# Weights of the second half split early and parked in DRAM, unrolled sequences, norms on ScalarE

## The reference

```python
x = x + attention(layernorm(x))     # q, k with rotary embedding, causal softmax, output weights wo
x = x + ffn(layernorm(x))
# ffn, for a token row x:
scores = softmax(x @ gate_w.T); topk_w, topk_idx = top_k(scores, 2)     # weights scaled to sum 1
y_all  = (silu(x @ w1[e]) * (x @ w3[e])) @ w2[e]                        # the two chosen experts
y      = sum(y_sel * topk_w) + (silu(x @ sw1) * (x @ sw3)) @ sw2        # plus the shared expert
```

## Time and profile before

| | us |
|---|---|
| three timed runs | 816.66, 817.6, 818.66 (median 817.6) |
| the profiled execution | 822.53, its span 820.8 |
| one sequence of the loop | 74.9 |
| busy share of the span | PE 92%, PEld 86%, DVE 78%, ACT 65%, POOL 59% |

### The profile page before, as it was taken

One profiled execution on the slowest core, in us unless ns is written; L12 is line 12 of the kernel. 1 busy time (PEld: TensorE's weight loads), 2 busy tenths in 40 slices (PEclk: granted clock), 3 DMA queues, 4 the chain that ended last, 5 costly groups with the idle time before them and its releaser, 6 DMA issues.

```text
span 820.8 us, 17064 instructions
## 1 busy us (share of the span) xinstructions
PE 755.2 (92%) x5520; PEld 703.7 (86%) x5520; DVE 640.8 (78%) x1765; ACT 532.9 (65%) x1663; POOL 482.2 (59%) x508
## 2 busy tenths in 40 slices
PE   3799999998999999999999999999996979999994
PEld 3688999988999999899989999998895868888884
DVE  5698989976997988799889979987995474444457
ACT  3688777756776777677667767777887433555531
POOL 3678666656667676766666676667776361343410
PEclk9899999998999999999999999999999997999998
DMA  7253434353000000000000000000232212333354
GB/s 223 58 178 114 160 168 183 153 206 116 15 2 27 0 13 6 19 13 0 13 13 13 0 26 0 13 6 22 83 80 79 74 40 78 110 105 108 113 209 144
DMA packets 35723, 61.20 MB, mean 75 GB/s; under 512 B 6744, under 2 KB 27192, under 8 KB 35096
## 3 DMA queue, kind: packets, MB, share of 16 engines
q1 hardware_dynamic: 31624, 49.14, 17.8%
q0 software_dynamic: 4048, 11.42, 3.9%
HBM read 47.03 MB, written 32.46 MB: 97 GB/s over the span
## 4 chain that ended last, share of the span: by engine, by line
PE 58%; DVE 17%; POOL 11%; issue 6%; ACT 4%; DMA 4%; SPq 0%; POOLq 0%; DVEq 0%; ACTq 0%
PE bank L528 45%; DVE work L879 5%; POOL work L425 4%; PE bank L568 3%; POOL qkt_lo L1416 3%; PE bank L561 3%; DVE work L872 2%; PE bank L577 2%; PE bank L728 2%; DVE work L888 2%; POOL rows_by_expert L1529 2%; DVE pt_lo L900 1%; DMA stage<-in_L_attn_wk 1%; DMA rows_by_expert<-xn,slot 1%; PE bank L743 1%
## 5 line engine op out<-in xcount | busy, mean ns | idle before, releaser
L1416 POOL TENSOR_TENSOR qkt_lo<-work,qkt_hi 128x512 fp32r<-128x512 f32 x128 | 165.6, 1294 | 99.9 <-ACT qkt_hi L1233 94.8
L425 POOL TENSOR_TENSOR work<-work 128x512 f32<-128x512 f32 x127 | 165.1, 1300 | 76.0 <-DVE work L879 71.2
L879 DVE TENSOR_TENSOR work<-bank,sinn 64x512 f32<-64x512 f32 x256 | 176.1, 688 | 3.4
L1233 ACT CAST qkt_hi<-work 128x512 fp32r<-128x512 f32 x128 | 79.5, 621 | 110.5 <-POOL work L425 109.8
L528 PE MATMUL bank<-xnt_hi,w_lo 128*128 128x256 f32 x512 | 146.9, 287 | 3.2 <-POOL w_lo L1476 3.0
L528 PE MATMUL bank<-xnt_lo,w_hi 128*128 128x256 f32 x512 | 146.6, 286 | 0.0
L528 PE MATMUL bank<-xnt_hi,w_hi 128*128 128x256 f32 x512 | 146.6, 286 | 0.0
L1240 ACT ACTIVATE work<-work,bias 128x128 f32<-128x128 f32 (+1 forms) x256 | 112.6, 441 | 0.0
L872 DVE TENSOR_TENSOR work<-bank,cosn 128x512 f32<-128x512 f32 x128 | 88.0, 687 | 23.5 <-PE bank L528 23.4
L528 PEld LDWEIGHTS bank<-xnt_hi,w_lo 128*128 128x128 f32 x512 | 99.7, 195 | 3.9 <-DVE xnt_lo L910 3.3
L528 PEld LDWEIGHTS bank<-xnt_hi,w_hi 128*128 128x128 f32 x512 | 100.0, 195 | 0.0
(11 more groups left out here) (151 smaller groups left out, 2181.7 us busy)
## 6 DMA issues: line engine op xcount, KB each, us to landing
rows_by_expert<-in_zero_t SPq DMA_DIRECT2D x8, 2056.0 KB
stage<-rows_by_expert SPq DMA_DIRECT2D x39, 128.5 KB, 2.1
stage<-in_L_ffn_w SPq DMA_DIRECT2D x32, 88.0 KB, 2.0
rows_by_expert<-in_zero_t SPq DMA_DIRECT2D x2, 1028.0 KB
resid<-in_L_attn_x SPq DMA_DIRECT2D x8, 256.0 KB, 3.9
stage<-in_L_attn_wq SPq DMA_DIRECT2D x8, 256.0 KB, 3.6
stage<-in_L_attn_wk SPq DMA_DIRECT2D x8, 256.0 KB, 4.3
stage<-in_L_attn_wv SPq DMA_DIRECT2D x8, 256.0 KB, 4.2
```

What stands on the lines that cost most here:

```text
L425: eng.tensor_tensor(roped[:, a], rope_cos[:, a], rope_sin[:, a], ALU.add).then_inc(rope_add, 1)
L879: op = nc.vector.tensor_tensor(rope_sin[lo:lo + 64, a], p_qk[a][hi:hi + 64, :, :], sn, ALU.mult)
L1233: nc.scalar.copy(qkt[a][0][:, :, :], roped[:, a]).then_inc(qkt_hi, 1)
L1416: nc.gpsimd.tensor_tensor(qkt[a][1][:, :, :], roped[:, a], qkt[a][0][:, :, :], ALU.subtract).then_inc(qkt_lo, 1)
```

## The change

- The 30 pieces of the second half's weights are split in sequences 0 to 5, one in each of the heads 10 to 14 of sequence 0 and of the heads 0, 1, 3, 4, 5 of sequences 1 to 5. The high and the low part go into two of the five staging slots (one buffer for each part), all low parts on POOL, and SP stores both into a DRAM tensor `w_d` (`keep`). ACT waits for the stores of a piece before it makes the high part of the next. The staging buffer has three slots for raw pieces then.
- In sequence 7 SP loads the split weights from `w_d` as the groups of attention weights become free.
- SP clears the scatter region once in each sequence.
- The loop is gone: sequences 1 to 7 are written out on all engines.
- Both norms are made on ACT, as `x * rstd + shift`, in head 9 and head 3. POOL makes `shift` behind its `rsqrt` in heads 6 and 2.
- Shared tiles 0 and 1 run in heads 12 to 15 of sequence 7, with the first product of tile 2. `S1` is 10, so tiles 3 to 9 come before the experts and 10 to 15 behind. Other PSUM banks are used; `silu` and product share a buffer. `finish` is called for two tiles in each late shared tile. Some `nop`s are dropped.

```diff
-S1 = 8
+S1 = 10
+        w_d = nc.dram_tensor("weights_split", (2, NU * DC + 2 + E, P, CH), F32, kind="Internal").ap()
+        parts = [stage[:, RAW + b, :].bitcast(F32R) for b in range(2)]
...
+            heads = [(FIRST, h) for h, k in enumerate([3, 2, 3] + [2] * 6) for _ in range(k)]
+            heads += [(FIRST, h) for h in range(10, N - 1)]
+            heads += [(b, h) for b in range(1, B - 2) for h in (0, 1, 3, 4, 5)]
...
+            def keep(k):
+                sp.wait_ge(w_lo[1], lo_count(NATT + k + 1, 1))
+                for b in range(2):
+                    sp.dma_start(w_d[b, k], stage[:, RAW + b, :]).then_inc(kept, 16)
+                if k % 5 == 4:
+                    b = k // 5 + 1
+                    sp.wait_ge(qk_ps, b * N + 4)
+                    clear(b)
...
 # ACT
             def split_hi(n):
                 _, seen = pieces[n]
-                act.wait_ge(staged[n % NSTAGE], staged_count[n])
+                if n == NATT:
+                    wait_pieces(act, NATT)
+                if n > NATT:
+                    act.wait_ge(kept, 32 * (n - NATT))
+                act.wait_ge(staged[slot_of(n)], staged_count[n])
...
+                        if h == 12:
+                            silu_s(0)
+                            rows_high(1)
...
+                        if h == 14:
+                            silu_s(1)
+                            high_s(0)
+                        if h == 15:
+                            silu_s(2)
+                            rows_high(3)
+                            high_s(1)
+                    elif h == 9:
+                        norm_x(b + 1)
                     if b is not FIRST:
+                        if h == 3:
+                            rows_norm(b, b - 1)
...
 # POOL
+            def shifts(k, done_sem, count, step_sem, n):
+                nc.gpsimd.tensor_scalar(shift[:, k, :], mv[:, :, 0], -1.0, 1.0, ALU.mult, ALU.mult).then_inc(step_sem, 1)
+                pool.wait_ge(step_sem, 2 * n - 1)
+                pool.wait_ge(done_sem, count)
+                nc.gpsimd.tensor_tensor(shift[:, k, :], shift[:, k, :], rstd[:, :], ALU.mult).then_inc(step_sem, 1)
...
 # PE, in the heads of the last sequence
-                    if b is LAST and h >= 14:
-                        up_s(0, h - 14)
+                    if b is LAST:
+                        if h == 12:
+                            up_s(0, 0)
+                        if h == 13:
+                            up_s(0, 1)
+                            up_s(1, 0)
+                        if h == 14:
+                            turn_s(0)
+                            up_s(1, 1)
+                        if h == 15:
+                            up_s(2, 0)
+                            turn_s(1)
...
-            sequence(1)
-            with pool.Fori(2, LAST) as b:
+            for b in range(1, B):
                 sequence(b)
-            sequence(LAST)
```

More of the change, by code:

```diff
@@ L167, in build @@
         assert DCONST <= D - 2 * NJ
-        room = work[:, e0:2816]
+        room = work[:, 2048:2816]
         past = room[:, 0:NJ * E].rearrange("p (j e) -> p j e", j=NJ)
@@ L411, in split_now @@
         def split_now(b, h):
-            which = "first" if b is FIRST else "last" if b is LAST else None
-            return plan.get((which, h), [])
-        FIRST, LAST = 0, B - 1
+            return plan.get((b, h), [])
         def wait(eng, s, value):
@@ new lines, in _, with units_in @@
+            for k in range(NP - NATT):
+                if k >= RAW:
+                    keep(k - RAW)
+                piece_in(NATT + k)
+            for k in range(NP - NATT - RAW, NP - NATT):
+                keep(k)
+            sp.wait_ge(qk_ps, (LAST - 1) * N + 4)
+            clear(B - 1)
+            clear(B)
+            sp.wait_ge(cleared, 16 * (B + 1))
+            sp.dma_start(xs_d[E * REGION:XROWS, :], zero_t[E * S:, :]).then_inc(cleared, 16)
+            def units_in(lo, hi, done):
+                for u in range(lo, hi):
+                    for b in range(2):
+                        src = w_d[b, DC * u:DC * (u + 1), :, 0:UW].rearrange("c p m -> p c m")
+                        sp.dma_start(ups[b][:, u].bitcast(F32), src).then_inc(done, 16)
@@ new lines, in free @@
+            def free(g):
+                sp.wait_ge(qk_ps, LAST * N + (g + 1) * GH)
+                sp.wait_ge(v_ps, LAST * 2 * G + 2 * (g + 1))
+            sp.wait_ge(kept, 32 * (NP - NATT))
+            free(0)
+            units_in(0, 2, ups_in)
+            rows_in(0)
+            units_in(2, 4, experts_in)
+            free(1)
+            units_in(4, 8, experts_in)
+            free(2)
+            units_in(8, NU, experts_in)
+            k0 = NU * DC
+            for b in range(2):
+                for n in range(SB):
+                    r = min(P, SI - n * P)
+                    src = w_d[b, k0 + n // 2, 0:r, n % 2 * D:(n % 2 + 1) * D]
+                    sp.dma_start(downs_s[b][0:r, n].bitcast(F32), src).then_inc(downs_in, 16)
@@ L483, in tile_in @@
+            k0 += 2
+            sp.wait_ge(rope_mul, B * N)
+            rows_in(1)
+            rows_in(2)
+            sp.wait_ge(s_ps, B * N)
+            rows_in(3)
+            free(3)
+            for b in range(2):
+                for k, r in ((0, P), (1, E_TAIL)):
+                    src = w_d[b, k0:k0 + E, 0:r, k * D:(k + 1) * D].rearrange("e p d -> p e d")
+                    sp.dma_start(downs_e[b][0:r, :, k, :].bitcast(F32), src).then_inc(experts_in, 16)
             def tile_in(j):
@@ L506, in _ @@
                 tile_in(j)
-            for t in range(S1, S1 + XSLOTS):
+            for t in range(S1, min(S1 + XSLOTS, NT)):
                 rows_in(t)
@@ L1150, in _ @@
             dve.wait_ge(route_in, 64)
-            sequence(1)
-            with dve.Fori(2, LAST) as b:
+            for b in range(1, B):
                 sequence(b)
-            sequence(LAST)
             residual(LAST)
@@ L1355, in _ @@
             sequence(FIRST)
-            sequence(1)
-            with act.Fori(2, LAST) as b:
+            for b in range(1, B):
                 sequence(b)
-            sequence(LAST)
-            for t in range(1, S1):
+            for t in range(3, S1):
+                if t == 4:
+                    logits(B, 1)
                 if t + 1 < S1:
@@ L1366, in _ @@
                 silu_s(t)
-                if t == 2:
+                if t == 3:
                     rows_turned(B, 1)
                 high_s(t - 1)
-                if t == 2:
-                    logits(B, 1)
-                if t >= 4:
-                    for n in plan["rest"][2 * (t - 4):2 * (t - 3)]:
-                        split_hi(n)
             high_s(S1 - 1)
@@ L1582, in _ @@
             store_turned(B, LAST)
-            for n in plan["rest"]:
-                split_lo(n)
             for j in range(NJ):
```

291 lines of the change are left out of this document (161 added, 130 removed).

## The result

The changed kernel takes 858.82 us (median of 4 runs, 856.68 to 861.57), the kernel before 817.30 us (4 runs, 816.66 to 818.66). The ratio is 1.0508, 95% interval 1.0472 to 1.0543. The forecast was 825 us in 800 to 845: the direction was right, the size was not. The profiled execution has a span of 859.7 us.

A forecast was written before the change was run, and what follows sets the result against it. TensorE was taken to set the pace. Store waits (+39.8) and shifts (+1.0) against savings of 5.6, 3.5, 2.5, 3.2, 2.0, 8.6 and 7.5 us gave +7.9 on the 817.6 us median: 825 us, range 800 to 845.

The forecast's parts named there:

- the sum of the waits: Sequences 0 to 5: PE waits in 19 gaps because ACT waits for store pairs, +39.8 us in all.
- the gap from head 4 to 5: Sequences 1 to 5: copies, low parts and stores in series take 7.45 us against PE's 4.43, so 3.0 us lost.
- 1 us, at most 3: POOL's two small shift operations in heads 2 and 6, priced for all sequences.
- rival 4: Stores land late because clears and loads share the queue, 1 us more per gap: 844 us; 0.17 together with rival 3.
- -5.6 us for the clears in a row: Sequence 1: without nine clears in a row its scatter lands like the others, saving 5.6 us.
- Residual add to first expert tile, -8.6: Second half: this stretch falls from 39.6 to 31 us, counting on the plan's slow step going away.
- The end, -7.5: Behind the experts: six shared tiles instead of eight, 30.8 us from reload to last add becomes 23.3.
- Sequence 7, -3.2 and -2.0: Heads 0 to 11 without splits save 3.2 us; heads 12 to 15 with the first shared tiles save 2.0.
- The loop, -2.5: Writing out the loop removes POOL's idle time at five turns, 0.5 us each.
- The norms, -3.5: Moving head 2's norm from VectorE to ACT removes PE's 0.46 us wait there in seven sequences.
- Rival 3, the clock: Waits in sequences 0 to 5 also lower PE's clock, 18 us more: 843 us; 0.17 together with rival 4.
- Rivals 1 and 2: Waits smaller than the second half's gain (812 us, chance 0.27); ACT's wait costs nothing (786 us, chance 0.09).

The follow-up runs named there:

- e12: The kernel before, profiled once more with no edit: 817.65 us (1 run).
- e6: As e5, with no two of the 30 kept splits in neighbouring heads: 798.82 us, ratio 0.9759.
- e3: Changed kernel with both norms back on VectorE at heads 9 and 2, without POOL's shifts and their waits: 856.36 us, ratio 1.0450.
- e1: Changed kernel with the splits of sequences 1 to 5 at heads 0, 2, 4, 7, 9: 816.16 us, ratio 1.0016.
- e2: Changed kernel with POOL making a kept piece's low part right behind the rope sum, before waiting for high q and k: 816.33 us, ratio 0.9988.
- e11: Changed kernel with only e5's early issue of the clears: 854.03 us, ratio 1.0438.
- e4: Kernel before with its loop over sequences 2 to 6 written out on all four engines: 813.97 us, ratio 0.9967.
- e5: As e2, with each clear issued right behind the fifth piece's stores, without its wait for the fourth q and k: 807.63 us, ratio 0.9881.
- e7: As e6, with e3's edit (both norms on VectorE, no shifts on POOL): 804.67 us, ratio 0.9838.
- e9: Changed kernel with a semaphore per store; ACT waits for the high store and POOL's subtraction, POOL for the low store: 819.43 us, ratio 1.0021.

## Why the prediction was wrong

By stages: up to the last residual add the forecast's terms add up to +24.0 us and behind it to -16.1. Against e12, which lacks the late scatter, the profiled execution has +54.1 (692.65 - 638.52) and -10.3. The larger miss is in the sequences.

Measured against e6, which has the same second half and no waits, the waits cost 123.92 - 114.97 = 9.0 us up to the first add, and then 13.5, 9.2, 8.6, 10.8 and 10.0 us in the five steps behind it: 61 us. The forecast had 39.8. The 61 may be some us too high, since the one profiled execution is 2.75 us above its median and e6's is 3.3 below; the medians differ by 60.0 us, and 4.9 us of the difference of the profiles lie behind the last add.

1. **The failed step: the sum of the waits, 5.9 us per sequence.** The price of a store pair (2.85 us) and the series were read rightly, and the gap from head 4 to 5 that was worked out as 7.45 us is 7.33 (copies at 320.33 and 327.66). By the first copies of each head against e12's, heads 4 and 5 of the five sequences together are 25.3 us longer, where the forecast had 23 and up to 2 for the wide pieces. Two things were left out.
   - I followed a wait up to TensorE and stopped. On an engine that works in order the late ScalarE makes POOL late too, and POOL has its own pieces and norm arithmetic to do before the next rope sum. Head 3 is longer by 0.9, 1.5, 2.4, 2.3 and 2.3 us in sequences 1 to 5, 9.5 us in all, booked as "1 us, at most 3". Of each, 0.6 us is there in sequence 6 too (5.67 us, and 4.97 in e3) and is the norm's. In sequence 3 it is 7.47 us, and 5.99 in e1, 6.57 in e2. That POOL is the way is read from its rows; e2 changed POOL's order and ScalarE's waits together, so no experiment shows it alone.
   - The clear "at a sequence's start, 50 us before the scatter" was held to be harmless. In sequence 1 it runs beside the stores of head 0, 7.1 us instead of 2.9; in sequences 2 to 5 it runs beside the last scatters of the sequence before, for which POOL waits in head 1 (1.52, 0.95, 0.66 and 1.06 us; no such wait in e11). Heads 1 and 2 together are longer by 7.4 us in sequence 1 and by 3.6, 2.1, 2.0 and 3.2 in the next four, 18.2 us against 6.5 in the forecast. The forecast saw the order of clear and stores, called it the clear's only cover, and gave it a price only in rival 4. e11 takes 4.8 us off for sequences 2 to 5.

   Heads 6 to 8 cancel: in sequence 3 head 6 is 1.3 us shorter, head 7 1.8 longer, head 8 0.5 shorter. The forecast's own sum has two small slips, 6.85 for 6.80 us and 2.5 for six times 0.45; they change nothing.
2. **The term that was no term: -5.6 us for the clears in a row.** It was a loss of the profiled execution and not of the median one, and the 8.63 us read as POOL's wait were the scatter's time to landing. By bringing the sum to the median as well (4.9 us off) I took it off twice. e4 and e12 show steps of 74.7 and 74.95 us with the clears where they were.
3. **Residual add to first expert tile, -8.6.** It was 37.7 us in the profiled execution, but 31.6 to 34.1 us in the ten experiments with the changed second half; 31 was the forecast. A part that the forecast left out is a wait of POOL for the last two scatters, which land 8.5 and 7.1 us after their issue while the split weights come back from `w_d` (DMA share 0.97 and 0.82). Its norm step for the last rows is late by that, and VectorE's norm and TensorE's turn of these rows wait for it:

```profile
697.07 0.19 POOL L1524 TENSOR_SCALAR vare<-mv 128x2 f32<-128x2 f32 x1 [6.16 <-DMA rows_by_expert<-xn,slot]
```

   This step begins 4.4 us behind the add here, 2.3 in e5 and 1.9 in e11, where POOL does not wait for a scatter and the stretch is shortest, 31.6. That is 2.5 us; and in the two windows from 700 to 710 another 3.4 us of clock are missing. Together they make up the difference of 6.1 to e11. The step of the plan went from 6.57 to 0.48 us once POOL's ten subtractions beside it were gone. The Trainium skill (SBUF — State Buffer, "SBUF: two separate sides") says that one of the two engines holds the shared port pair for a whole instruction and the other blocks; the trace agrees that VectorE's step stood still beside POOL's work, but it did so for 6.57 us, beside nine or ten subtractions of 0.7 to 0.8 us each and not beside one.
4. **The end, -7.5:** measured -6.0. **Sequence 7, -3.2 and -2.0:** measured -5.1 for both, -5.2 against e12. **The loop, -2.5:** e4 has -3.1 and its interval touches none. **The norms, -3.5:** -5.9 beside spread splits (e7 to e6), 0.2 us in a sequence that splits nothing (sequence 6 in the changed kernel and e3), and in the changed kernel as a whole no gain can be told (e3). The same edit has three prices, by what stands beside it.
5. **Rival 3, the clock.** TensorE's clock was below 0.9 in ten windows of 5 us between 100 and 480 us in the changed kernel; e12 and e6 have none there. What is missing to full clock in these ten windows adds up to 14.6 us, an estimate of the most that it can have cost, where the rival had 18. Part of it cost nothing. Head 5 of sequences 2 and 3 is one stretch at full clock and one at 0.77, with the same length, because the series with the stores sets it (us, PE, PEld, DVE, ACT, POOL busy, clock, DMA share, GB/s):

```profile
237.62:244.94 7.32, 5.49 (x42) 5.02 (x42) 4.19 (x13) 4.03 (x14) 4.08 (x4) 1.00 0.39 132
320.73:328.05 7.32, 5.67 (x35) 5.67 (x36) 4.19 (x13) 4.03 (x14) 4.07 (x4) 0.77 0.35 121
```

   So it is real, but second, and it comes and goes with the waits; its share between 0 and 14.6 us stays open. Rival 4 was right for head 1 of sequence 1 alone. Rivals 1 and 2 were wrong.

## What to carry to other kernels

A wait added to an engine that works in order must be followed through every engine that it makes late, until one has slack, and not only to the first one that the bound engine waits for. Where a buffer is reused behind a store, spacing the users by two turns (e1), or giving each half its own semaphore (e9), was worth 43 and 39 us here; with all users spaced, the low part first and the clears early, the change turned from 5.1% slower to 2.4% faster (e6). And a large wait in one profile is a term only if the median run has it too: compare the profiled execution's own time with the median first.

## What the runs showed of the hardware

- From the issue of a pair of 256 KB stores from SBUF to the copy that waits for them it is 2.9 us in most gaps of the changed kernel. With a 2,056 KB write issued 7 to 10 us ahead on the same queue it is 7.1 us (changed kernel, sequence 1) and 4.8 to 8.5 us (e2); with that write issued some 13 us ahead it is 2.9 us again (changed kernel, sequence 3).
- Waits of the same length on TensorE (2.28 and 2.30 us, same place, same matmuls behind) were followed by a granted clock of 0.51 in one kernel and of 1.00 in another. The Trainium skill (TensorE: Matmul & The Clock Gate, "Why this matters for your kernels") advises against idle gaps between bursts of matmuls, because the clock falls; it means longer gaps than these two, of which one was followed by a fall all the same.
- Scatters of POOL land in 2.6 us (median, kernel before); the last two of sequence 7 in the changed kernel took 8.5 and 7.1 us while the weights were loaded from DRAM. One landed 8.63 us after its issue in one execution of the kernel before and kept POOL idle for 4.45 us; in another POOL does not wait at that place. The two executions differ by 0.6% in time.
- A low granted clock (0.77 over one head) did not lengthen a head that waits for its stores (7.32 us with it and without it).
